# Gates from the unnormalised projection, four band buffers and the last chunk's norm in the feed-forward: an audio-tower block in fp32 on one core

## What is computed

```python
h = xf @ W_proj + b_proj
res = h
y = _layernorm(h, ln_g, ln_b)
w = (y @ W_wgen + b_wgen).reshape(B, folded_T, HEADS, KSIZE)
w = jax.nn.softmax(w, axis=-1)
yp = jnp.pad(y, ((0, 0), (PAD_L, 0), (0, 0)))
taps = jnp.stack([yp[:, k:k + folded_T] for k in range(KSIZE)], axis=0)
taps = taps.reshape(KSIZE, B, folded_T, HEADS, R)
conv = jnp.einsum('kbthr,bthk->bthr', taps, w).reshape(B, folded_T, D)
out = res + jax.nn.relu(conv @ W_ff + b_ff)
```

## Time and profile before

| | |
|---|---|
| Three runs | 1167.72, 1172.85 and 1178.63 us; median 1172.85 |
| The profiled execution | 1165.51 us, of which 1163.7 us are the span of instructions |
| PE busy | 1085.1 us, 93% of the span |
| DVE, ACT, POOL busy | 574.6, 462.0, 423.0 us |
| Granted TensorE clock, mean | 0.965 of full |
| DMA | 127.18 MB, mean 109 GB/s |

### The profile page before, as it was taken

One profiled execution on the slowest core, in us unless ns is written; L12 is line 12 of the kernel. 1 busy time (PEld: TensorE's weight loads), 2 busy tenths in 40 slices (PEclk: granted clock), 3 DMA queues, 4 the chain that ended last, 5 costly groups with the idle time before them and its releaser, 6 DMA issues.

```text
span 1163.7 us, 14038 instructions
## 1 busy us (share of the span) xinstructions
PE 1085.1 (93%) x5056; PEld 817.4 (70%) x5056; DVE 574.6 (49%) x849; ACT 462.0 (40%) x758; POOL 423.0 (36%) x335
## 2 busy tenths in 40 slices
PE   7999997869899999998899999999999998999996
PEld 6878786757778788876688888888887774444442
DVE  5212174495435314436573673671745677454440
ACT  6233244534352524433342442341332325565442
POOL 2242424274111025433513513500253876354221
PEclk9989898889899999999899999999999898999999
DMA  8513310726436164362002002002147645123211
GB/s 296 185 69 145 113 50 31 208 91 166 145 134 177 37 147 142 117 207 95 1 19 91 10 10 90 9 19 82 46 127 262 235 181 198 64 91 119 71 46 45
DMA packets 70027, 127.18 MB, mean 109 GB/s; under 512 B 28361, under 2 KB 29385, under 8 KB 66257
## 3 DMA queue, kind: packets, MB, share of 16 engines
q1 hardware_dynamic: 63808, 109.48, 29.0%
q0 software_dynamic: 5120, 16.78, 4.3%
q10 hardware_dynamic: 1040, 0.16, 0.1%
HBM read 86.18 MB, written 40.22 MB: 109 GB/s over the span
## 4 chain that ended last, share of the span: by engine, by line
PE 68%; issue 8%; POOL 7%; DVE 6%; DMA 6%; ACT 3%; SPq 0%; POOLq 0%; ACTq 0%; DVEq 0%
PE bank L337 14%; PE bank L339 13%; PE bank L338 13%; PE bank L1886 10%; PE bank L1869 5%; POOL vacc L373 3%; PE bank L1768 3%; DMA band_s<-wk 2%; PE bank L1606 2%; DVE sq L415 2%; DVE db L1187 2%; DMA band<-band_s 2%; PE bank L1746 1%; PE bank L1593 1%; PE bank L1585 1%
## 5 line engine op out<-in xcount | busy, mean ns | idle before, releaser
L1886 PE MATMUL bank<-gt,dn_f 128*128 128x512 f32 x256 | 128.8, 628 | 0.0
L337 PE MATMUL bank<-xa_h,wp_h 128*128 128x512 f32 x256 | 105.7, 413 | 7.8 <-DVE xa_l L1160 7.1
L373 POOL TENSOR_TENSOR vacc<-vacc,sq 128x512 f32<-128x512 f32 x66 | 94.5, 1431 | 38.1 <-ACT sq L419 30.3
L337 PE MATMUL bank<-cv_h,wf_h 128*128 128x512 f32 x256 | 105.2, 411 | 0.8 <-ACT lg L885 0.8
L338 PE MATMUL bank<-xa_l,wp_h 128*128 128x512 f32 x256 | 103.4, 404 | 0.0
L339 PE MATMUL bank<-xa_h,wp_l 128*128 128x512 f32 x256 | 103.2, 403 | 0.0
L339 PE MATMUL bank<-cv_h,wf_l 128*128 128x512 f32 x256 | 101.4, 396 | 0.0
L338 PE MATMUL bank<-cv_l,wf_h 128*128 128x512 f32 x256 | 101.3, 396 | 0.0
L731 POOL TENSOR_TENSOR fo<-fo,res 128x512 f32<-128x512 f32 x32 | 41.9, 1319 | 157.8 <-ACT fo L904 121.3
L1133 ACT ACTIVATE gt<-bank 128x512 f32<-128x512 f32 x128 | 72.9, 593 | 46.3 <-PE bank L1886 46.1
L1886 PEld LDWEIGHTS bank<-gt,dn_f 128*128 128x128 f32 x256 | 44.3, 192 | 55.3 <-issue 37.2
(11 more groups left out here) (168 smaller groups left out, 2526.5 us busy)
## 6 DMA issues: line engine op xcount, KB each, us to landing
xs<-x_t SPq DMA_DIRECT2D x32, 256.0 KB, 5.9
h_s<-ho SPq DMA_DIRECT2D x8, 1024.0 KB, 3.8
db<-h_s SPq DMA_DIRECT2D x4, 2048.0 KB, 8.7
res<-h_s SPq DMA_DIRECT2D x32, 256.0 KB, 4.1
h_s<-fo SPq DMA_DIRECT2D x32, 256.0 KB, 2.5
dc<-h_s SPq DMA_DIRECT2D x4, 2048.0 KB, 9.4
h<-h_s SPq DMA_DIRECT2D x8, 1024.0 KB, 8.5
h_s<-h SPq DMA_DIRECT2D x8, 1024.0 KB, 4.8
```

Of the source, the lines that this page charges most:

```text
L337: pe.matmul(o, wh, xh, start=start, stop=False)
L373: g.tensor_tensor(vacc[:, :], t[:, 0, :] if k == 1 else vacc[:, :], t[:, k % 2, :], ALU.add).then_inc(ln_pool, 1)
L1886: mm = pe.matmul(o, dn_f[:, n, :], gt[:, i, :], start=i == 0, stop=i == FFB - 1)
```

## The change

Gate logits are computed from h itself. With W' = g*W, its column mean taken off each row, y @ W = rstd * (h @ W') + b @ W, so neither mean nor rstd is needed before the product. The new parts: wgs (g*W), the matmuls of gate_weights and gate_bias on PE in step 0 that centre it and make the constant c_bc, and in gates one multiplication by rstd and one addition of c_bc. The gate blocks of chunks 0, 1 and 2 now stand in projection steps 1, 2 and 3, one behind each k of group 0, and read ho. The gates of chunk 3 are made in feed-forward step 1. There are four zeroed band buffers in HBM, one per chunk, each zeroed by two DMAs of about 1 MB. yb is gone (the bias is added in place), db_late holds chunk 3 and db_next chunks 1 and 2. Chunk 3's mean, centres, squares and variance move from the stretch between the stages into feed-forward steps 0 and 1; its sum is made by DVE (late_sum) and not by POOL. Loops are written out.

```diff
+        wgs = place("wgs", [P, KB, LOGITS], F32, LNT + 8 * KIB)
+        c_bc = place("c_bc", [P, LOGITS], F32, CONST + 6688)
+        ccol = place("ccol", [P, 1], F32, CONST + 6848)
+        diagc = place("diagc", [P, LOGITS], F32, CONST + 6880)
...
-        db = place("db", [P, KB, N], F32, R1)
-        yb = place("yb", [P, KB, N], F32, R1 + 16 * KIB)
+        db_late = place("db_late", [P, KB, N], F32, R1)
+        db_next = place("db_next", [P, KB, N], F32, R1 + 16 * KIB)
+        db = [db0, db_next, db_next, db_late]
...
-                tokens = vacc[:, :].rearrange("q (p t) -> q t p", t=TILES)[:, t, :]
+                if L < CH:
+                    tokens = vacc[:, t * P:(t + 1) * P]
+                else:
+                    tokens = vacc[:, :].rearrange("q (p t) -> q t p", t=TILES)[:, t, :]
...
+                for g in range(2):
+                    sp.wait_ge(a_st[g], 16 * (n + 1))
+                if n in (1, 3):
+                    sp.wait_ge(a_mm, CH * KB)
+                elif n == 2:
+                    sp.wait_ge(yt_mm, KB * n)
+                sp.dma_start(db[n][:, :, :], h0_s[n]).then_inc(b_ld[n], 16)
...
             for c in range(CH):
                 if c + 1 < CH:
                     a_load(c + 1)
+                    band_zero(c + 1)
+                if c == CH - 1:
+                    b_load(0)
                 if c > 0:
                     stat_store(c - 1, 0)
-                    if c < CH - 1:
-                        stat_store(c - 1, 1)
-                if c == CH - 2:
-                    b_load(0)
+                    stat_store(c - 1, 1)
+                    band_skew(c - 1)
+                if c == CH - 1:
+                    band_load(0)
                 a_store(c, 0)
-                if c == CH - 1:
-                    band_skew(0)
-                    band_load(0)
-                    stat_store(c - 1, 1)
                 a_store(c, 1)
 
+            for u in range(U_FF + 4, U_FF + 8):
+                unit_load(sp, u)
+            band_load(1)
             b_load(1)
-            stat_store(CH - 1, 0)
-            for u in range(U_FF + 4, U_V):
+            for u in range(U_FF + 8, U_FF + 12):
                 unit_load(sp, u)
-            stat_store(CH - 1, 1)
+            b_load(3)
+            for u in range(U_FF + 12, U_V):
...
+            def a_stats(n):
+                y_high(n, 0, ho)
+                y_high(n, 1, ho)
+                y_high(n, 2, ho)
+                stat_copy_act(act, n, n)
+                for k in range(KB):
+                    stat_square_act(act, n, k)
+                    if k + 3 < KB:
+                        y_high(n, k + 3, ho)
+                gate_logits(n)
+
+            def a_step(c):
+                if c > 0:
+                    a_stats(c - 1)
+                a_evac(c, A_GROUPS[0])
+                if c == 0:
+                    act.wait_ge(wg_cent, 2)
+                    act.activation(wg[:, :, 0, :], wgs[:, :, :], ACT.Copy).then_inc(wg_hi, 1)
+                else:
+                    stat_std_act(act, c - 1)
+                    gate_exp(c - 1)
+                a_evac(c, A_GROUPS[1])
...
+                if c == CH - 1:
+                    for k in range(KB):
+                        y_base(0, k)
...
+            act.wait_ge(a_lo, KB * CH)
             for u in range(U_FF, U_FF + 4):
                 unit_hi(act, u)
...
+                first = c == 0
                 if first:
-                    act.wait_ge(ln_pool, 14 * CH)
-                for k in range(KB if ahead else 0):
-                    y_base(c + 1, k)
-                    y_high(c + 1, k)
-                    if first:
+                    for k in range(KB):
+                        y_base(1, k)
                         unit_hi(act, U_FF + 8 + k)
-                if ahead:
-                    gate_logits(c + 1)
...
+                if c == 1:
+                    ln_std_act(act, CH - 1, lambda e: None)
+                    for k in range(KB):
+                        act.wait_ge(xh_sc, k + 1)
+                        y_high(CH - 1, k, db_late)
...
                 ff_relu(c, 0)
+                ff_relu(c, 1)
+                ff_relu(c, 2)
...
                 if first:
-                    act.wait_ge(mean_st, 16 * CH)
-                ff_relu(c, 1)
-                if ahead:
-                    gate_exp(c + 1)
-                ff_relu(c, 2)
+                    for k in range(KB):
+                        ln_square_act(act, CH - 1, k, db_late[:, k, :])
+                if c == 1:
+                    for k in range(KB):
+                        y_base(2, k)
+                    gate_logits(CH - 1)
+                    gate_exp(CH - 1)
...
             for k in range(KB):
-                a_low(1, k)
-            with v.Fori(0, CH - 2) as c:
-                a_stats(c)
-                for k in range(KB):
-                    a_low(c + 2, k)
-
+                v.tensor_scalar(out=wgs[:, k, :], in0=wg_raw[:, k, :], scalar1=vec[:, LN_G + k:LN_G + k + 1],
+                                scalar2=None, op0=ALU.mult).then_inc(wg_ok, 1)
...
-            def y_low(n, k):
-                since(v, y_b, n, 8, k + 1)
+            def y_low(n, k, src):
                 since(v, yr_hi, n, 8, k + 1)
-                src = yb0 if isinstance(n, int) and n == 0 else yb
+                since(v, yr_used, n, 8, k - 1)
                 v.tensor_tensor(yr_l[:, k % 2, :], src[:, k, :], yr_h[:, k % 2, :].bitcast(F32),
                                 ALU.subtract).then_inc(yr_lo, 1)
...
+                if n < CH - 1:
+                    v.wait_ge(ln_rstd, n + 1)
+                    v.tensor_tensor(tiled, turned, rstd4[:, :].unsqueeze(2).unsqueeze(3)
+                                    .to_broadcast([P, TILES, CONV_HEADS, TAPS]), ALU.mult).then_inc(sm5, 1)
...
+            def a_stats(n):
+                for k in range(3):
+                    y_low(n, k, ho)
+                for k in range(KB):
+                    stat_center(v, n, n, k, ho[:, k, :])
+                    if k + 3 < KB:
+                        y_low(n, k + 3, ho)
+                stat_recip_dve(v, n)
+                gates(n)
+
+            for c in range(CH):
+                if c > 0:
+                    a_stats(c - 1)
+                if c + 1 < CH:
+                    for k in range(KB):
+                        a_low(c + 1, k)
+            y_prep(0)
...
+            def late_sum():
+                v.wait_ge(b_ld[CH - 1], 16)
+                for k in range(1, KB):
+                    if k > 1:
+                        v.wait_ge(ln_pool, 14 * (CH - 1) + k - 1)
+                    v.tensor_tensor(acc[:, :], db_late[:, 0, :] if k == 1 else acc[:, :], db_late[:, k, :],
+                                    ALU.add).then_inc(ln_pool, 1)
+
+            def b_step(c):
+                if c == 0:
+                    y_prep(1)
+                    late_sum()
+                    for k in range(KB):
+                        ln_center_dve(v, CH - 1, k, db_late[:, k, :], db_late[:, k, :])
+                if c == 1:
+                    ln_rstd_dve(v, CH - 1)
+                    v.wait_ge(ln_sq, 8 * CH)
+                    for k in range(KB):
+                        v.tensor_tensor(db_late[:, k, :], db_late[:, k, :], rstd[:, :], ALU.mult).then_inc(xh_sc, 1)
+                        if k > 0:
+                            y_low(CH - 1, k - 1, db_late)
+                    y_low(CH - 1, KB - 1, db_late)
+                    y_prep(2)
+                    gates(CH - 1)
...
+            def gate_weights():
+
+                pe.wait_ge(wg_ok, 16 + KB)
+                pe.wait_ge(masks_ok, 17)
+                for k in range(KB):
+                    pe.matmul(bank[7][:, 0:LOGITS], mean_w[:, :], wgs[:, k, :], start=k == 0, stop=k == KB - 1)
+                for k in range(KB):
+                    mm = pe.matmul(bank[7][0:LOGITS, 64:65], wg_raw[:, k, :], vec[:, LN_B + k:LN_B + k + 1],
+                                   start=k == 0, stop=k == KB - 1)
+                mm.then_inc(wg_mm, 1)
+
+            def gate_bias():
+                pe.wait_ge(wg_cent, 3)
+                pe.matmul(bank[7][:, 128:128 + LOGITS], mean_w[0:LOGITS, :], diagc[0:LOGITS, :],
+                          start=True, stop=True).then_inc(wg_mm, 1)
+
...
+                        if c == 0:
+                            if (g, k) == (0, 7):
+                                gate_weights()
+                            if (g, k) == (1, 3):
+                                gate_bias()
+                            continue
+                        if g == 0:
+                            gate_block(c - 1, k)
+                        if (g, k) == (0, 2):
+                            pe.wait_ge(a_ev, 8 * c)
                             stat_mean_pe(pe, c - 1)
-                        if later and (g, k) == (1, 1):
+                        if (g, k) == (1, 1):
                             stat_var_pe(pe, c - 1, c - 1)
...
```

(30 more changed lines are left out.)

429 lines of the change are left out of this document (170 added, 259 removed).

## The result

| | before | after |
|---|---|---|
| Median of seven runs, us | 1172.10 | 1180.99 |
| Range, us | 1167.72 to 1178.63 | 1178.23 to 1183.18 |
| Ratio | | 1.0071 (95%: 1.0048 to 1.0093) |
| The profiled execution, us | 1165.51 | 1180.99 |
| Its span, us | 1163.7 | 1179.3 |

The changed kernel is slower by 0.7%. That is clear of noise and less than the 1.2% of the prediction's likeliest case; of the three cases of the prediction the one that came true is the middle one, within 1%, which I had given 0.32; slower by more than 1% had 0.55.

The account below looks back on a forecast made before the run. The prediction took PE as the bound, delayed by waits and a slow clock. Its terms, stretch by stretch from projection step 0 to feed-forward step 3, summed to +14.6 us, giving 1187 against 1172.85, range 1166 to 1203.

Parts of the forecast that it names:

- the prediction's likeliest case: Whole kernel: slower by more than one per cent, over 1184.6 us, with 1187 as the forecast; chance 0.55.
- the middle one: Whole kernel: within one per cent of no change, between 1161 and 1184.6 us; chance 0.32.
- wgs in step 0: Projection step 0: gate_weights on PE waits 2.3 us for wgs, ready at 27.9 us after eight small DVE operations.
- block 0: Projection steps 1 and 2: first gate block, due at +2.0 us, goes at +4.0 behind POOL's ho additions; wait 1.9.
- block 3: Projection steps 1 and 2: due at 11.9 us, its low part ready at 13.7 behind mean and first centre; wait 1.8.
- wf_l at i = 8: Feed-forward step 0: PE waits 13.7 us for unit 8's low part, late behind chunk 1's load and preparation.
- the logits: Feed-forward step 1: chunk 3's logits stand behind eight bias additions on ACT; PE waits 9.5 us at the turn.
- The ring: Projection steps: centre, square, y_high, y_low take 3.2 us per k against PE's 2.5, since y_low waits for POOL's addition.
- Rival B: Projection steps: the chain keeps up, waits fall from 7.7 to 4; -4.5 in each of three steps, 1173 us; chance 0.18.
- rival E: Each projection step falls to the lower clock twice: +3.4 us in three steps, 1197; within the 0.55 for slower.
- The clock: Slow PE clock after new waits of 1.5 us or more: 1 to 2.2 us each, 1.5 in projection step 0.
- Rival C: Feed-forward step 0: chunk 1 lands before T+7, PE never waits for unit 8; -16 us, 1171; chance 0.14.

Follow-up runs that it names:

- small_add: Changed kernel with POOL's second to seventh additions of squares per chunk cut to 8 of 512 columns in three projection steps; 1167.43 us in one execution.
- load_first: Changed kernel with chunk 1's h and statistics loaded ahead of w_ff units 4 to 7 on SP's queue; 1165.90 us, ratio to before 0.9954.
- all_fixed_2: Changed kernel with all projection and feed-forward order edits, centres reading PSUM, and chunk 3's squares 4 to 7 later on ACT; 1119.19 us, ratio to before 0.9553.
- swap_shift: Changed kernel with DVE's next centre ahead of yr_l and gate blocks one k later on PE, in gate-making projection steps; 1163.99 us in one execution.
- prep_pairs: Changed kernel with chunk 1's centres and scales interleaved on DVE in feed-forward step 0; 1181.65 us in one execution.
- weights_late: Changed kernel with gate_weights and gate_bias placed later on PE in projection step 0; 1175.38 us, ratio to before 1.0044.

## Why the prediction was right, and where not

**The places.** PE waited where the text put it, and for what it named: wgs in step 0 (2.3 forecast, 2.8), block 0 (1.9; 1.7), block 3 (1.8; 1.3), the four later blocks (0.7 each; 0.5), the variance (1.2; 1.2), wf_l at i = 8 (13.7; 16.7), the logits (9.5; 9.1). Block 3's wait was shorter because PE came to it 12.6 us after the step's start and not 11.9; the chain of centre, square, yr_h and yr_l took the 2.6 forecast.

**The ring.** The rule of turns carried the two projection steps: the pitch was 3.18 to 3.19 against 3.2 forecast, and small_add showed the cause by 2.51 without the additions. The rule of the Trainium skill (SBUF — State Buffer, Who interferes with whom), that the loser of the two waits to the end, agrees with the trace: 1.37 us beside an addition for 0.69 alone. Rival B, that the chain keeps up, fell by 0.7 us a k; rival E, two falls of the clock in each projection step, did not come either (PEclk 1.00, 1.00 and 0.97). What I had not seen is that the order on DVE decides it and costs nothing to change: behind the next centre, yr_l waits for an addition while ACT already squares.

**The clock.** Charged at 1 us for each of steps 1 to 3, it cost nothing in steps 1 and 2 (PEclk 1.00, though three waits are longer than 1.1 us, one 1.74) and 1.6 in step 3. In step 0 it cost 4.5 us (2.2 in the passes and 2.3 behind them) where 1.5 was charged; at the full clock the passes are 2.6, not the 4 that I took. With 0.5 more of wait and the 0.1 that is left for gate_bias, which I had left out, that is the 2.2 us by which step 0 was missed.

**Feed-forward step 0.** Near in total (+1.1 for -0.8) by luck, from terms that were off. h, mt and rt landed at T+21.2 (forecast T+20.3), the first scale was done at T+26.8 (forecast T+27.1), but unit 8's low part took 5.01 us where I had 1.7, and PE went on at T+33.3. The wait of 3.6 at the mean did not come, since PE reached it at T+43.0 (forecast T+40.4) and the sum was done at T+42.2 (forecast T+44); the relu's wait was 5.1 for 3. Rival C, h landing before T+7, fell with its premise: its load was issued at T+7.5, behind POOL's first low parts. load_first made C true, and gained 15.1 us against the changed kernel's median, near the 16 that C was priced at.

**The sum and the median.** The sum was +14.6 and the two profiled executions differ by 15.5. That is closer than the terms deserve: the stretches were missed by +2.2 to -0.9 us, and the misses partly cancel, which is luck. The prediction of 1187 came out 6 us too high because I added the 7.3 us by which the kernel before's profiled execution lay under its median. The changed kernel's profiled execution is its median, and the medians differ by 8.9. There is one trace of the kernel before, so I cannot say in which stretch its slower executions lose time. From the last matmul of the feed-forward to the end all kernels do the same, and this stretch alone took from 660.1 us (all_fixed_2) to 666.2 (swap_shift) in the fourteen traces (662.1 in the kernel before, 662.9 in the changed one). A difference worked out on one trace belongs to that trace; where its execution lies off the median, both bases are possible, and the one I took was the worse.

## What to carry to other kernels

A change that moves work to an earlier stage is priced by the queue that it enters there: in this kernel three orders, an h load behind four weight loads, logits behind eight bias additions, a low part ahead of a centre, held back 34 us by the runs that undid them one at a time (15.1, 6.5 and, from one execution, 12.6), more than the whole difference between the two kernels. When a wait is removed, ask which one stood hidden behind it (prep_pairs: 6.3 us less at unit 8, and 9.4 at the mean, 4.0 of which had been hidden) and look at the order again, since the gain only shows when the last of them is gone. And compare a profile with the median of the other kernel only after asking whether the execution was a typical one.

## What the runs showed of the hardware that was not expected

Two low parts of the same size on POOL, each beside a DVE stream of two-input operations, took 5.01 us in one kernel and 1.64 in another. In the first, DVE's scales beside it kept their full pace (0.67 us each); in the second DVE and POOL took turns. Centres that read the mean in PSUM left each projection step 1.0 us shorter than centres that read it in SBUF (50.12 and 51.14 in step 2).

A wait of 2.83 us in projection step 0 went with a clock at half (matmuls of 0.63 us up to 37 us), and without the wait, in weights_late, that was gone. Waits of up to 1.74 us in projection steps 1 and 2 of the changed kernel left the clock at 1.00, but the same waits in step 3 did not (PEclk 0.97), nor did they in step 1 of weights_late, and in the kernel before the wait of 1.51 us for the variance was followed by half. So in these traces the length of one wait does not tell by itself whether the clock falls.
